# First attention of a two-layer block on one core: token normalisation, low halves and transposes back, placed one to two units later in two queues

## What is computed

```python
q, k, v = heads(x @ Wq.T), heads(x @ Wk.T), heads(x @ Wv.T)      # 16 heads of 16
q, k = _layernorm(q, gq, bq), _layernorm(k, gk, bk)
scores = where(causal, einsum('nhld,nhmd->nhlm', q, k), NEG)
out = einsum('nhlm,nhmd->nhld', softmax(scores), v)
x = x + out.reshape(N, L, EMB) @ Wo.T + bo
```

## Time and profile before

| what | value |
|---|---|
| median of 3 runs | 4406.71 us |
| the profiled execution, its own time | 4404.48 us |
| its span in the trace | 4402.5 us |
| TensorE (PE) busy | 3607.0 us, 82% |
| VectorE (DVE) busy | 3065.4 us, 70% |
| ScalarE (ACT) busy | 2207.7 us, 50% |
| GpSimd (POOL) busy | 699.3 us, 16% |
| mean granted TensorE clock | 0.892 |

### The profile page before, as it was taken

How to read it: one execution, slowest core, us unless ns; L and a number is a source line. 1 busy time by engine, 2 the same in 40 slices (tenths; PEclk the granted TensorE clock), 3 DMA queues, 4 the chain that set the end, 5 groups by cost and what they waited for, 6 DMA issues and landing times.

```text
span 4402.5 us, 91305 instructions
## 1 busy us (share of the span) xinstructions
PE 3607.0 (82%) x31136; PEld 2831.7 (64%) x31136; DVE 3065.4 (70%) x6460; ACT 2207.7 (50%) x5290; POOL 699.3 (16%) x839
## 2 busy tenths in 40 slices
PE   3797887978879788797988879788797887978878
PEld 2576665756657566675666757666576665756657
DVE  4677676777767777676776767767677676777766
ACT  2455544555445554445545445554455544555444
POOL 1111121011110121111211101112011121012110
PEclk9898988988889898898988989988898898989989
DMA  2000000000000000000000000000000000000000
GB/s 68 6 2 7 6 6 6 2 7 6 6 6 2 7 6 6 6 7 2 5 7 6 7 6 1 7 6 6 6 2 7 6 6 6 1 7 6 6 1 6
DMA packets 33856, 30.33 MB, mean 7 GB/s; under 512 B 8816, under 2 KB 33264, under 8 KB 33328
## 3 DMA queue, kind: packets, MB, share of 16 engines
q1 hardware_dynamic: 33328, 23.68, 1.8%
HBM read 15.28 MB, written 8.39 MB: 5 GB/s over the span
## 4 chain that ended last, share of the span: by engine, by line
PE 62%; DVE 14%; issue 13%; POOL 5%; ACT 4%; SPq 1%; DVEq 0%; POOLq 0%; ACTq 0%; DMA 0%
PE bank L630 14%; PE scores L764 9%; PE bank L641 8%; PE scores L617 5%; PE scores L613 4%; PE bank L776 4%; PE scores L618 4%; PE scores L619 3%; DVE negmax L1108 3%; PE bank L601 2%; POOL qf L508 2%; PE scores L738 2%; PE scores L667 1%; DVE x L1309 1%; DVE res L1222 1%
## 5 line engine op out<-in xcount | busy, mean ns | idle before, releaser
L881 ACT ACTIVATE prob<-scores,negmax 128x128 f32<-128x128 f32 (+3 forms) x2048 | 991.8, 532 | 386.5 <-DVE negmax L1108 354.1
L1108 DVE TENSOR_REDUCE negmax<-scores 128x1 f32<-128x128 f32 (+3 forms) x2048 | 887.1, 485 | 106.9 <-PE scores L619 91.0
L630 PE MATMUL bank<-ident,prob 128*128 128x128 f32 x5120 | 794.2, 296 | 182.5 <-DVE probt L1116 180.1
L1116 DVE COPY probt<-bank 128x512 f32<-128x512 f32 x896 | 603.8, 688 | 273.4 <-PE bank L630 267.2
L630 PEld LDWEIGHTS bank<-ident,prob 128*128 128x128 f32 x5120 | 602.1, 151 | 295.8 <-DVE probt L1116 205.3
L619 PE MATMUL scores<-mask,ident 128*128 128x128 bf16 x2048 | 466.0, 240 | 0.0
L617 PE MATMUL scores<-khh,qt 128*128 128x256 f32 (+2 forms) x1024 | 434.6, 425 | 13.3 <-ACT qt L851 8.3
L851 ACT ACTIVATE probt<-bank 128x512 f32<-128x512 f32 x384 | 230.3, 600 | 359.1 <-PE bank L630 359.1
L458 POOL TENSOR_TENSOR rstd<-var,expo 128x4 f32<-128x4 f32 x64 | 67.0, 1053 | 2159.2 <-DVE var L1236 1430.0
L613 PE MATMUL scores<-qkt 96*128 96x128 bf16 (+3 forms) x1024 | 287.1, 339 | 78.6 <-ACT prob L881 64.3
L618 PE MATMUL scores<-kll,qt 128*128 128x256 f32 (+2 forms) x1024 | 343.5, 335 | 0.0
(11 more groups left out here) (187 smaller groups left out, 6719.9 us busy)
## 6 DMA issues: line engine op xcount, KB each, us to landing
x_in<-in_x_rows SPq DMA_DIRECT2D x16, 512.0 KB, 3.3
out_rows<-x SPq DMA_DIRECT2D x16, 512.0 KB, 3.7
r_gu<-in_wg SPq DMA_DIRECT2D x2, 512.0 KB, 4.7
r_gu<-in_wu SPq DMA_DIRECT2D x2, 512.0 KB, 5.2
r_d<-in_wd SPq DMA_DIRECT2D x1, 1024.0 KB, 6.6
r_wqt<-in_wq_nope_t SPq DMA_DIRECT2D x1, 512.0 KB, 6.5
r_wqr<-in_wq SPq DMA_DIRECT2D x2, 256.0 KB, 8.7
r_wob<-in_wo SPq DMA_DIRECT2D x1, 512.0 KB, 4.9
```

What stands on the lines that cost most here:

```text
L630: ins = nc.tensor.transpose(bank[4 + n % 2][:, q * P:(q + 1) * P], prob[:, u % 2, q, i * P:(i + 1) * P], ident[:, :])
L881: nc.scalar.activation(prob[:, u % 2, q, 0:n], bank[q][:, 0:n], ACT.Exp, bias=negmax[:, a, u, q:q + 1], **row_sums).then_inc(prob_ready.se ...
L1108: nc.vector.tensor_reduce(negmax[:, a, u, M * part:M * part + M], scores[:, M * part:M * part + M, 0:n], axis=AX.X, op=ALU.max, negate=Tru ...
L1116: nc.vector.tensor_copy(probt[:, u % 2, i], bank[4 + n % 2][:, :]).then_inc(probt_dve.sem, 1)
```

## The change

Nothing is added or removed. In iterations of the first attention, some calls stand later. On TensorE `transpose_out(g)` goes from iteration 4g+6 to 4g+7, and `transpose_tok(0)` from 12 to 13. On ScalarE `split_first(0)` goes from 12 to 13. On VectorE `normalise_first(g)` goes from 4g+6 to 4g+8 for g = 0, 1, 2 (the last in the extra iteration 16), and `low_first(0)` from 12 to 14. The calls behind the loop stay.

```diff
@@ TensorE, attend
-                    if a == 0 and u % NT == 2 and u > NT:
+                    if a == 0 and u % NT == 3 and u > NT:
                         transpose_out(b, u // NT - 1)
-                    if a == 0 and u == 3 * NT:
+                    if a == 0 and u == 3 * NT + 1:
                         transpose_tok(b, 0)
@@ VectorE, attend
-                if a == 0 and u % NT == 2 and u > NT:
-                    normalise_first(b, u // NT - 1)
-                if a == 0 and u == 3 * NT:
+                if a == 0 and u % NT == 0 and u > NT + 1:
+                    normalise_first(b, u // NT - 2)
+                if a == 0 and u == 3 * NT + 2:
                     low_first(b, 0)
```

## The result

The changed kernel takes 4142.34 us (median of 4 runs, 4132.88 to 4146.17) against 4406.49 us before: a ratio of 0.9398 with a 95% interval of 0.9381 to 0.9415. The forecast was 4164 us, with a range of 4130 to 4265. The profiled execution took 4139.4 us, 265.1 less than the one before, or 16.6 us in a batch where 15.2 were forecast.

A forecast was written before the change was run, and what follows sets the result against it. Hand-overs bound the kernel, VectorE's waits stopping the whole machine. Steps of 54.68 us fall to 39.45, 15.2 a batch; sixteen batches give 243 us, so 4404.5 becomes 4161, and 4164 us with the median's 2.2; range 4130 to 4265.

The forecast's parts named there:

- VectorE's waits are the machine's waits: First attention, iterations 6, 10, 12, 14: VectorE's stalls hold up TensorE and ScalarE too, 11.18 us a batch.
- The steps: Eight intervals from unit 6's maxima to unit 15's last copy, mostly between units' maxima: 54.68 us becomes 39.45 a batch.
- The step 13 to 15: From the maxima of unit 13 to those of unit 15: 10.17 us before, 6.5 after.
- ScalarE's high half: Iteration 13, ahead of the exponentials of unit 14: costs between 0 and 3.08 us, taken as 0.4.
- 9 to 11: From the maxima of unit 9 to those of unit 11: 8.10 us before, 1.93 + 3.07 = 5.00 after.
- The last step: From the maxima of unit 15 to the last copy: 8.52 us before, 7.3 after.
- The price of the moved work: In steps 8 to 9 and 12 to 13: transposes back add 0.49 us, normalisation 0.63, each at full price.
- The clock's part: First attention's stage: TensorE's higher clock gives 5.8 us of the 15.2 gained in a batch.
- the stalls' own part: First attention's stage: removed stalls less the price of moved work, without any clock gain, 9.4 us a batch.
- the clock stays low: Rival: stalls go, but small gaps of TensorE keep its clock low; 9.4 us a batch, 4256 us; 18%.
- The full payback of the low clock: Rival: all 16.7 us at half pace is on the path, giving 8.4 beside 9.4 us; 4122 us; 8%.
- a wait of over 1 us with late exponentials: Sign of being wrong: ScalarE waits over 1 us before `o1h` in iteration 13, the exponentials behind it late.

The follow-up runs named there:

- the first run: Changed kernel with transposes of the tokens, high half and low half left in iteration 12: 4180.64 us.
- the fourth: Changed kernel with VectorE's in-loop normalisation one iteration later (4g+7) than in the kernel before, not two: 4290.4 us.
- eighth run: Changed kernel with the normalisation put ahead of the last copy of its iteration: 4127.35 us.
- the fill: Kernel before, stalls kept, with twenty identity transposes on TensorE in each of iterations 6, 10 and 14: 4297.79 us.
- the second measurement: The changed kernel measured once more, unaltered: 4131.15 us.
- both moves in the gaps: Changed kernel, normalisation ahead of its iteration's last copy, transposes back between the two late blocks of iteration 4g+6: 4123.39 us.
- transposes doubled: Changed kernel with the four transposes back made twice for groups 0 to 2: 4175.7 us.

## Why the prediction was right

- **VectorE's waits are the machine's waits.** Shown. The stage gave 54.86 - 38.58 = 16.3 us a batch of the 16.6 measured, and putting waits back (one in the first run, three in the fourth) put their time back.
- **The steps.** Seven of eight came within 0.22 us, taken over from the undisturbed units of the earlier trace rows. The step 13 to 15 was mis-sized: 5.73 in place of 6.5 us. ScalarE's high half, taken at 0.4, cost nothing that can be seen. Most of the rest is the pattern of 9 to 11, which came out 0.22 us shorter than 1.93 + 3.07 both there and in 13 to 15. In the changed kernel ScalarE has no wait ahead of `copy_out` in iteration 9, where the undisturbed unit 5 had one of 0.19; with the normalisation in the gap (eighth run) the step takes 5.02. So it is the normalisation ahead of the step that shortens it, and gives back a third of its own price; that ScalarE's wait is the reason is argued from the one row. The last step was 0.2 us too short in the forecast. (The sum itself: 4161 and 2.2 are 4163, not 4164.)
- **The price of the moved work.** Right in the stage: 0.63 and 0.49 forecast, and the doubled pieces cost 0.33 (of 0.34) and 0.43 us (of 0.49) in their places. Put into the gaps both became free there (8 to 9 then takes 3.73 us), though 9 to 11 and 13 to 15 took 0.25 and 0.31 more.
- **The clock's part.** Forecast as 5.8 us of the 15.2, measured alone as 6.6 in the stage, or 7.1 by the estimate above if it had stayed up in every batch. So this term was too small by 0.8 to 1.3 us, and the stalls' own part is 9.2 to 9.7, against 9.4. The kernel before had a mean clock of 0.88 over 69.8 us, which makes 16.8 us at half pace. The rule of the Trainium skill (page "TensorE: Matmul & The Clock Gate", section "HAM oscillation — how this bites in real kernels"), half the throttled time, gives 8.4 of it. The measured 6.6 to 7.1 lies between the two, and neither is clearly nearer: most of the slow time was on the path, but not all. One reading behind this term was loose: the transposes in the earlier trace rows take 0.88 us for 0.60, which is not half the pace, as the granted clock is still 1.00 from 1222.40 to 1222.90 and falls while they run.
- **Rivals.** That the clock stays low fell by the row with 1.00 in the stage. The full payback of the low clock (17.8 us in a batch, 4122 us) fell by the fill, 6.6 to 7.1 us in place of 8.4, and by the 16.3 us of the stage; it was the nearest rival, and the second measurement (4131 us) is nearer to it than to 4164. ScalarE did stand before the high half, 1.43 us in place of 2.48:
```profile
1175.85 0.60 ACT L851 ACTIVATE o1h<-bank 128x512 fp32r<-128x512 f32 x1 [1.43 <-PE bank L658]
1176.35 1.99 ACT L881 ACTIVATE prob<-scores,negmax 128x384 f32<-128x384 f32 x4
```
The exponentials of unit 14 behind it did start late: VectorE's first maximum of that unit was done at 1174.31, 2.0 us before. The prediction had named this, a wait of over 1 us with late exponentials, as a sign that it is wrong. The sign came and cost nothing that can be seen: VectorE had its copy of 1176.38 and the low half to do, and went on to the maxima of unit 15 at 1177.58 without idle time.
- **Not foreseen** was that stages which the change doesn't touch move by up to 2 us from batch to batch, and up to 1.7 us in the mean of a run, with their clock. For the change itself that came to little (44.13 to 43.57 us behind the stage), but it is as large as the finer steps that were tried after it.

## What to carry to other kernels

Where one engine's consumer stands in the same turn of a software pipeline as its producer on another engine, and the producer itself needs that engine's last result, the consumer waits by construction: put it so far behind that the producer's own queue order proves it done, and look for a gap already there to put it into. Price such a move by units of the same loop that have no such stall. And judge small gains by the stage as well as by the whole, since the whole also holds what TensorE's clock does in the next stage.

## What was not expected of the hardware

Idle time of TensorE costs twice. Twenty transposes whose result nobody reads, put into each of three stands of some 3.4 us, made the kernel before 104 us (2.3%) faster without removing any of VectorE's waits. Fourteen of them ahead of the projections of the second attention took 50 us off another kernel, but only 10 off the changed one, whose clock there was at 0.91 already.

A stretch of identical code took 43.05, 43.57, 44.69 and 44.78 us a batch in four measurements (the changed one twice, both moves in the gaps, transposes doubled); the mean granted clock of its 16 batches was 0.914, 0.887, 0.834 and 0.833, so low clock and long time go together. Within one execution it is the same: some 43.0 us at 0.92 in eleven batches, 45.0 at 0.80 in four. Two kernels that differ by 2.0 us a batch in one stage thus ended 8 us apart and not 32. Why one batch or one kernel gets the lower clock there and another not, with the same code in the stretch, stays open: no run varied the moment at which the stand begins and nothing else.
